# A second buffer for x, column sums moved from TensorE to VectorE for one group, and two warm-up products dropped

## The reference

```
q_emb = relu(cond @ W3 + b3)                   # 32 x 512
v_sum = sum of x over the 64 rows of a batch
h0    = relu(((n*x + v_sum) * q_emb) @ W2 + b2)   # 2048 rows of 512
w1    = ternary(W_fc)     # 2048 x 512: sign, or 0, times the mean |w| of 64 neighbours
h     = square(relu(h0 @ w1.T))                # 2048 rows of 2048
hn    = h * rsqrt(mean(h*h) + eps)
out   = x + hn @ ternary(W_proj).T
```

## Time and profile before

| what | value |
|---|---|
| median of three runs | 321.33 us |
| the profiled execution: its own time | 321.12 us |
| the profiled execution: span of the trace | 319.1 us |
| TensorE (PE) matmuls busy | 313.4 us, 98% |
| VectorE (DVE) busy | 210.6 us, 66% |
| ScalarE (ACT) busy | 192.1 us, 60% |
| GpSimd (POOL) busy | 113.0 us, 35% |
| stage 1 on TensorE, first unit to last | 11.88 to 77.77 us |

### The profile page before, as it was taken

One profiled execution on the slowest core, in us unless ns is written; L12 is line 12 of the kernel. 1 busy time (PEld: TensorE's weight loads), 2 busy tenths in 40 slices (PEclk: granted clock), 3 DMA queues, 4 the chain that ended last, 5 costly groups with the idle time before them and its releaser, 6 DMA issues.

```text
span 319.1 us, 3835 instructions
## 1 busy us (share of the span) xinstructions
PE 313.4 (98%) x1326; PEld 238.8 (75%) x1326; DVE 210.6 (66%) x290; ACT 192.1 (60%) x282; POOL 113.0 (35%) x94
## 2 busy tenths in 40 slices
PE   8999999999999999999999999999999999999995
PEld 7664746545888788888888888888888888888884
DVE  0539989788888846676556655755655675665555
ACT  1658988799996884455544454644455554445550
POOL 1004333333733535413344431344433314433330
PEclk9999999999999999999999999999999999999999
DMA  6994959489521110016000000600000034000003
GB/s 190 358 279 111 286 138 291 108 191 275 73 49 34 33 36 1 0 46 219 0 0 2 0 0 0 244 23 0 0 2 0 0 116 149 0 0 2 0 1 133
DMA packets 31331, 27.02 MB, mean 85 GB/s; under 512 B 18736, under 2 KB 20816, under 8 KB 31312
## 3 DMA queue, kind: packets, MB, share of 16 engines
q1 hardware_dynamic: 29984, 26.25, 28.9%
q10 hardware_dynamic: 1328, 0.53, 0.7%
HBM read 18.39 MB, written 4.19 MB: 71 GB/s over the span
## 4 chain that ended last, share of the span: by engine, by line
PE 90%; ACT 4%; issue 3%; DVE 2%; POOL 0%; POOLq 0%; DVEq 0%; ACTq 0%
PE ps_out L320 34%; PE ps_acc L308 32%; PE ps_acc L292 17%; PE ps_out L273 5%; ACT x_t L568 1%; ACT x_t L565 1%; PE ps_acc L362 1%; DVE abs_sum L412 1%; DVE y_hi L452 1%; PE ps_x L377 1%; PE ps_acc L369 0%; ACT w_scale L532 0%; ACT w_t L545 0%; ACT w_abs L526 0%; PE ps_x L352 0%
## 5 line engine op out<-in xcount | busy, mean ns | idle before, releaser
L210 POOL TENSOR_TENSOR wv_sb<-wv_sb 128x512 f32<-128x512 f32 x55 | 82.2, 1494 | 114.1 <-ACT wv_sb L571 114.1
L320 PE MATMUL ps_out<-w_t,y_hi 128*128 128x512 f32 x256 | 101.7, 397 | 0.2 <-DVE y_lo L454 0.2
L320 PE MATMUL ps_out<-w_t,y_lo 128*128 128x512 f32 x256 | 101.0, 394 | 0.0
L308 PE MATMUL ps_acc<-h_hi,w_t 128*128 128x512 f32 x256 | 100.1, 391 | 0.0
L308 PE MATMUL ps_acc<-h_lo,w_t 128*128 128x512 f32 x256 | 100.0, 391 | 0.0
L454 DVE TENSOR_TENSOR y_lo<-x_t,y_hi 128x512 fp32r<-128x512 f32 x64 | 91.3, 1427 | 2.2
L565 ACT ACTIVATE x_t<-ps_acc 128x512 f32<-128x512 f32 x64 | 38.1, 595 | 81.1 <-PE ps_acc L308 81.0
L452 DVE CAST y_hi<-x_t 128x512 fp32r<-128x512 f32 x64 | 29.2, 457 | 73.6 <-PE ps_out L320 65.8
L320 PEld LDWEIGHTS ps_out<-w_t,y_hi 128*128 128x128 f32 x256 | 48.1, 188 | 11.5 <-DVE y_lo L454 0.6
L320 PEld LDWEIGHTS ps_out<-w_t,y_lo 128*128 128x128 f32 x256 | 48.4, 189 | 10.9
L308 PEld LDWEIGHTS ps_acc<-h_hi,w_t 128*128 128x128 f32 x256 | 48.3, 189 | 10.6 <-issue 0.2
(11 more groups left out here) (49 smaller groups left out, 147.5 us busy)
## 6 DMA issues: line engine op xcount, KB each, us to landing
x_sb<-in_x_dram SPq DMA_DIRECT2D x7, 1024.0 KB, 5.8
raw<-in_L_ffn_W_fc_dram SPq DMA_DIRECT2D x8, 512.0 KB, 5.3
raw<-in_L_ffn_W_proj_dram SPq DMA_DIRECT2D x8, 512.0 KB, 6.1
out_dram<-x_t SPq DMA_DIRECT2D x16, 256.0 KB, 2.1
x_sb<-in_x_dram SPq DMA_DIRECT2D x4, 256.0 KB, 5.5
wv_sb<-in_L_cond_W_dram SPq DMA_DIRECT2D x4, 256.0 KB, 7.1
x_t<-in_L_cond_W_dram ACTq DMA_DIRECT2D x1, 512.0 KB, 4.6
w_turned<-w_tern SPq DMA_TRANSPOSE x16, 3.1
```

The lines of the kernel that those rows point to most:

```text
L210: engine.tensor_tensor(sq_acc[:], sq_acc[:], y_sq[:, v % SQ_RING, :], ALU.add).then_inc(sq_added, 1)
L308: last = pe.matmul(ps_acc[:, (UNITS + v) % ACC_RING, :], w_t[:, j, k * P:(k + 1) * P], part[:, k, g * BANK:(g + 1) * BANK], start=(k == 0 ...
L320: last = pe.matmul(ps_out[:, t, :], part[:, v % RING, t * P:(t + 1) * P], w, start=(j == 0 and part is y_hi), stop=(j == HJ - 1 and part i ...
```

## The change

Group 3 and group 1 get a home of their own for x, `x_odd`. Its space is that of the split y of stage 2 (`y_split`, which now holds both `y_hi` and `y_lo`). `load_x(g)` therefore waits for the sums of group g-2 and not g-1, and each home has a semaphore. The order of loads changes: `load_x(1)` stands behind `load_wv(3)` and `load_pair(2)` and not ahead of them, `load_x(2)` behind turn 0 and not turn 1, `load_x(3)` behind turn 3 and not turn 4.

For group 3, TensorE only transposes the 16 blocks of x, ahead of unit 8 and not of unit 10. VectorE makes n*x + v_sum itself: for each k it reduces the 64 columns of every batch, multiplies by n and adds, and multiplies by q_emb as before. It does this for one k behind the rounding in each of the units 8 to 11, where before it did all four k in unit 10.

Steps 5 and 6 move from units 7 and 8 to 6 and 7, step 10 from unit 13 to 14. The two products after the transposes of cond go.

```diff
-    STEP_AT_UNIT = {0: 0, 1: 1, 3: 2, 4: 3, 5: 4, 7: 5, 8: 6, 9: 7, 11: 8, 12: 9, 13: 10, 15: 11}
+    STEP_AT_UNIT = {0: 0, 1: 1, 3: 2, 4: 3, 5: 4, 6: 5, 7: 6, 9: 7, 11: 8, 12: 9, 14: 10, 15: 11}
+    def sums_by_vector(g):
+        return g == GROUPS - 1
...
+        batch_sum = sb("batch_sum", [P, GB], F32)
-        y_hi = sb("y_hi", [P, RING, BANK], F32R)
-        y_lo = sb("y_lo", [P, RING, BANK], F32R)
+        with nc.sbuf_tensor("x_odd", [P, TT, D], F32) as x_odd:
+            pass
+        y_split = sb("y_split", [P, 2 * RING, BANK], F32R)
...
             def load_x(g):
-                sp.wait_ge(xt_done, KD * g)
-                sp.dma_start(x_sb[:], x_rows[g]).then_inc(x_loaded, 16)
+                wait(sp, xt_done, KD * (g - 1))
+                sp.dma_start(x_of[g % 2], x_rows[g]).then_inc(x_loaded[g % 2], 16)
...
             load_wv(2)
-            load_x(1)
             load_wv(3)
             load_pair(2)
+            load_x(1)
             load_pair(3)
...
-                if i == 1:
+                if i == 0:
                     load_x(2)
-                if i == 4:
+                if i == 3:
                     load_x(3)
...
                     for t in range(TT):
-                        last = sum_x_block(t, k)
+                        if sums_by_vector(g):
+                            last = pe.transpose(ps_out[:, k, t * P:(t + 1) * P], x_of[g % 2][:, t, k * P:(k + 1) * P], ident_f[:])
+                        else:
+                            last = sum_x_block(g, t, k)
...
-            for i in range(2):
-                pe.matmul(ps_acc[:, 1, 0:P], ident_f[:], ident_f[:], start=True, stop=True)
...
-                if u % KD == SUMS_AT and u // KD + 1 < GROUPS:
+                if u % KD == SUMS_AT and u // KD + 1 < GROUPS - 1:
                     sum_x(u // KD + 1)
+                if u == KD * (GROUPS - 2):
+                    sum_x(GROUPS - 1)
                 make_h0(u)
...
+                src = ps_out[:, k, :].rearrange("p (b n) -> p b n", n=N)
+                if sums_by_vector(g):
+                    at = 2 * (KD * [v for v in range(GROUPS) if sums_by_vector(v)].index(g) + k)
+                    wait(dve, summed, at)
+                    dve.tensor_reduce(batch_sum[:], src, AX.X, ALU.add).then_inc(summed, 1)
+                    dve.wait_ge(summed, at + 1)
+                    dve.scalar_tensor_tensor(out=x1, in0=src, scalar=float(N),
+                                             in1=batch_sum[:].rearrange("p (b o) -> p b o", o=1).to_broadcast([P, GB, N]),
+                                             op0=ALU.mult, op1=ALU.add).then_inc(summed, 1)
+                    dve.wait_ge(summed, at + 2)
+                    src = x1
...
-                if g + 1 < GROUPS and m == SUMS_AT:
+                if g + 1 < GROUPS - 1 and m == SUMS_AT:
                     for k in range(KD):
                         scale_x(g + 1, k)
+                if g == GROUPS - 2:
+                    scale_x(g + 1, m)
```

More of the change, by code:

```diff
@@ L126, in adaln_ffn @@
         cond_t = h0_f[:, 1, 0:KQ * BATCHES].rearrange("p (k b) -> p k b", k=KQ)
+        y_hi = y_split[:, 0:RING, :]
+        y_lo = y_split[:, RING:2 * RING, :]
+        x_of = [x_sb[:], x_odd[:]]
         x_res = x_sb
@@ L152, in adaln_ffn @@
         x0_loaded = [sem(f"x0_loaded{t}") for t in range(TT)]
-        x_loaded = sem("x_loaded")
+        x_loaded = [sem(f"x_loaded{i}") for i in range(2)]
         res_loaded = sem("res_loaded")
@@ L160, in adaln_ffn @@
         xt_done = sem("xt_done")
+        summed = sem("summed")
         x1_ready = sem("x1_ready")
@@ L229, in load_x @@
             def load_x(g):
-                sp.wait_ge(xt_done, KD * g)
-                sp.dma_start(x_sb[:], x_rows[g]).then_inc(x_loaded, 16)
+                wait(sp, xt_done, KD * (g - 1))
+                sp.dma_start(x_of[g % 2], x_rows[g]).then_inc(x_loaded[g % 2], 16)
             def load_res(g):
                 if g == 0:
-                    sp.wait_ge(xt_done, KD * GROUPS)
+                    sp.wait_ge(xt_done, KD * (GROUPS - 1))
                 else:
@@ L271, in _, with sum_x_block @@
         def _(pe):
-            def sum_x_block(t, k):
-                return pe.matmul(ps_out[:, k, t * P:(t + 1) * P], x_sb[:, t, k * P:(k + 1) * P], sum_mat[:],
+            def sum_x_block(g, t, k):
+                return pe.matmul(ps_out[:, k, t * P:(t + 1) * P], x_of[g % 2][:, t, k * P:(k + 1) * P], sum_mat[:],
                                  start=True, stop=True)
             def sum_x(g):
-                pe.wait_ge(x_loaded, 16 * g)
+                pe.wait_ge(x_loaded[g % 2], 16 * ((g + 1) // 2))
                 pe.wait_ge(x1_ready, KD * g)
@@ L381, in _ @@
                 for k in range(KD):
-                    last = sum_x_block(t, k)
+                    last = sum_x_block(0, t, k)
                     if t == TT - 1:
@@ L438, in scale_x @@
                 x1 = x1_t[:, g % RING, k, :].rearrange("p (b n) -> p b n", n=N)
-                dve.tensor_tensor(x1, ps_out[:, k, :].rearrange("p (b n) -> p b n", n=N),
+                src = ps_out[:, k, :].rearrange("p (b n) -> p b n", n=N)
[9 more added lines that the diff above has]
+                    src = x1
+                dve.tensor_tensor(x1, src,
                                   q_t[:, k, g * GB:(g + 1) * GB].rearrange("p (b o) -> p b o", o=1).to_broadcast([P, GB, N]),
```

## The result

The changed kernel takes 324.84 us (median of five runs), the kernel before 321.29 (five runs beside them): ratio 1.0133, 95% interval 1.0078 to 1.0187. The forecast was 323.4: the direction is right and the range holds it, but of the 3.5 us it has 2.1.

The account below looks back on a forecast made before the run. TensorE and a second chain over ScalarE and VectorE both bound the kernel; TensorE's 0.35 and 1.8 us gained and 1.2 lost are overtaken by that chain's +2.1 us, giving 323.4 us, range 320.9 to 325.0.

Parts of the forecast that it names:

- TensorE and a second chain are both at the bound: Up to 105.54 us: ScalarE and VectorE's ReLU, square, split and weight steps have no slack and hand on +2.1 us.
- VectorE's sums: Group 3, units 8 to 11: 2.12 us for each k, 8.5 us where 2.4 stood, 6.1 us more.
- Transposes: Group 3's sums on TensorE: 16 one-record transposes replace 32 records, taking 1.8 us and saving 1.8 us.
- Loads: x of group 1 lands last, at 19.8 us; TensorE wants it at 18.63 and stands still for 1.2 us.
- Nothing of the gain survives: Early weight pair 2 ends ScalarE's 3.41 us wait, but the ReLU of unit 2 comes 0.9 us later; worth nothing.
- Warm-up products: Start of the kernel: dropping the two products gains 0.35 us at the end of the first sums, bounds 0 and 0.85.
- rival 3: TensorE itself slower, by a late rate change or transposes that don't overlap: +2.9 to +4.5 us, chance 0.10.
- All later terms are TensorE's and unchanged: After the second chain's delay at 105.54 us, the rest of stage 2 adds nothing.
- theory A: Set up after the result: without the warm-up products TensorE's rate sometimes changes late, which makes the long runs.

Follow-up runs that it names:

- e1: The changed kernel run again with no edit, for a second profile: 324.95 us.
- e5: The changed kernel with the two warm-up products put back and batch_sum declared behind all other arrays: 322.88 us, ratio 1.0056.
- e7: e5 with x of group 1 loaded ahead of the last quarter of W and weight pair 2: 324.02 us, ratio 1.0091.
- e3: The kernel before with only the two warm-up products dropped: twelve runs, median 321.74 us, four of them at 324.48 to 325.34.
- e2: The changed kernel with the two warm-up products put back: 324.8 us, ratio 1.0106.
- e8: e5 with the sums of group 3 made by products on TensorE again: 322.38 us, ratio 1.0038.
- e12: e5 with the load order weight pair 2, x of group 1, last quarter of W: 322.34 us, ratio 1.0027.
- e11: e12 with weight step 11 moved from stage 1 to stage 2, later steps and the last two copies shifted: 319.79 us, ratio 0.9939.
- e4: The kernel before with only the change's memory layout (batch_sum ahead, y_hi and y_lo in one array): 323.27 us, ratio 1.006.
- e6: The kernel before with 32 empty bytes ahead of its first array, so every array moves: 321.35 us, ratio 0.9996.

## Why the prediction was right and where it was wrong

- **TensorE and a second chain are both at the bound**: right, and the step on which the direction rests. e1 and e5 have the ReLU of unit 15 at 81.2 and the first of stage 2 at 81.8, to a tenth of what was forecast. That this delay is handed on holds, too: the projection that starts at 105.54 us before starts at 107.66 in e1 and e5, 2.12 later. e5, which is the change without its two other effects, costs 1.8 us by the ratio where 2.1 were forecast. The hit to a tenth is in part luck: in e1 the ReLU of unit 2 came 0.3 us earlier than forecast (26.73), the wait for turned weights was 1.16 us and not 0.6, and the four k of VectorE took 0.3 us less, and these cancel.
- **VectorE's sums**: right. 2.12 us were forecast for each k. VectorE's timeline of e1 for one k (start us, us):

```profile
54.74 0.68 DVE L457 TENSOR_REDUCE batch_sum<-ps_out 128x8 f32<-128x512 f32 x1
55.46 0.69 DVE L459 SCALAR_TENSOR_TENSOR x_t<-ps_out,batch_sum 128x512 f32<-128x512 f32 x1
56.18 0.69 DVE L464 TENSOR_TENSOR x_t<-x_t,q_t 128x512 f32<-128x512 f32 x1
```

From 54.74 to the next operation at 56.79 it is 2.05 us. ScalarE waited for the scale of pair 9 at 66.41 as forecast for 66.3.

- **Transposes**: one record each, 16 of them. TensorE's timeline of the changed kernel:

```profile
50.86 1.91 PE L293 MATMUL ps_out<-ident_f,x_odd 128*128 128x128 f32 x16
52.60 1.88 PE L306 MATMUL ps_acc<-x_t,wv_sb 128*128 128x512 f32 x4
```

1.74 us from start to start against 1.8 forecast. The Trainium skill (TensorE: Matmul & The Clock Gate, Part 4: PE-mode transpose) gives some 275 ns in a kernel's context for a transpose of 128x128 in bf16. Each float32 record here lasts 272 ns, but they follow each other at 109 ns, so here such a figure is a duration and not a pace, as the prediction read it.

- **Loads**: half right. x of group 1 does land last, but at 19.4 us and not 19.8, and in e1 TensorE asks at 19.25 and not 18.63, so it waited 0.2 us (0.6 with the warm-up, e5) instead of 1.2. "Nothing of the gain survives", said of the early pair 2, was wrong: e7 shows that it carries 1.4 us through ScalarE's steps to the last ReLU. That the sum came out right for stage 1 all the same is luck.
- **Warm-up products**: 0.35 us of gain were forecast, 0.14 came in e3, and in the changed kernel a loss of 0.4 to 0.5 (e1 against e2 and e5). The late change of rate was part of rival 3, which had 0.10; it is real, in two of seven runs of the changed kernel, e1 counted in, and four of twelve of e3, and costs 2.7 to 3.4 us when it comes in the one (3.5 to 4.3 in e3, against 321.0). By the means it adds 1.0 us (325.75 against 324.71 for the four short ones). The argument against it was that TensorE stays busy "but for a few tenths"; 0.59 us of gap were there in the long run, and the rate stayed low.
- **The step that failed: "All later terms are TensorE's and unchanged".** They were TensorE's, but not unchanged: from 107.66 us on, where TensorE alone is the bound, a full group takes 0.65 us longer, and what is left of stage 2 from there adds up to +1.9 us, by the spans of e1 and e5 as by the medians of e2 and e5. This term the sum put at nothing. Moving y by 32 bytes was in the diff in plain sight, as a line that declares `batch_sum`, and I gave it no price, because I priced instructions and waits only. With this term the forecast would have been 325.3, against 324.84.

The pieces, by medians: stage 1 +1.8 (e5), the place of y +1.9 (e2 less e5), dropping the warm-up 0 in short runs (324.84 and 324.8) and about 3 in the others. Of the stage-1 part, 0.5 are the sums on VectorE (e5 less e8) and 0.5 to 0.9 the late load (e5 less e12); what is left was not taken apart further. e11 shows that the second chain was one step over.

## What to carry to other kernels

Where two chains meet at the end of a stage, work taken off the one and put on the other is a loss unless the other is relieved in the same edit: the same change that cost 1.8 us gained about 2 us (e11, with its loads reordered) when one weight step went to the next stage. Follow such a chain through the queues, and give an early load what it is worth down to the end of the stage. When an array is added, look where the operands of the hot loop come to lie, and try a few places as one tries buffer counts; and judge a cut in the warm-up by a dozen runs, since a kind that comes in one run of three can be missed in five.

## What the runs showed of the hardware that was not expected

The place of the split y against the other arrays moves the pace of TensorE's 512-column products by up to 2.6% (58.25 to 59.75 us for a group, 318.4 to 323.3 us for the whole) with the same instructions, and the products that do not read y (L308: 391 to 395 ns in e4) slow down, too. Moving everything together does nothing (e6). That two engines' accesses to one memory meet more or less often (VectorE writes y while TensorE reads) would fit, but it was not tested, and no rule over the six places of y was found. The Trainium skill (SBUF — State Buffer, section "SBUF: two separate sides") says that engines contend only at the port that VectorE and GpSimd share. By it VectorE's writes would not slow TensorE's reads directly; no run here shows whether the pace comes by way of it, since GpSimd adds the squares all through stage 2.

TensorE's records tell a rate that the granted clock does not. The granted clock is printed as full, the 2.4 GHz level, in this stretch of the changed kernel (the columns are us, TensorE busy and records, granted clock, DMA share, GB/s), while the sums in it take 421 ns a record and follow each other at the half pace, as the 1.2 GHz level would give:

```profile
7.00:14.00 7.00, 7.00 (x33) 1.00 1.09 351
```

e1 does 45 records in the same stretch. What TensorE did before: it stood still for 0.59 us up to 6.99 in the one, 0.20 up to 6.59 in the other, and in both its records still took 421 ns when the gap came. In e1 they shortened at about 7.4 us; in the long run TensorE was then busy without a gap, and its records shortened only at about 16.6 us, from 714 to 1073 ns to 592 for the products of L306. e3's profiled run stood still for 0.86 us and went on at the full rate, but it had that rate before the gap. So a longer gap at the low rate, as in theory A, fits all three, with one long run profiled; it was not tested, and what decides stays open.

SyncE's issues themselves take longer while many loads are under way: in e1 a load of W issued at 4.48 us took 0.47 us to issue, the two from 5.62 us on 3.40 together and the load of weights behind them 1.42, so that x of group 1, which waits for nothing, was issued at 10.53 us and landed 8.86 us later. What holds the issues up, a full queue or another limit, no run here shows.
